# A two-layer deformable convolution kernel: bias sums and image 0's moves in another order, left columns copied by ACT, and one addition moved from POOL to DVE

## The reference, cut to what matters

```
x = x + L0(gn(x))      # L0: a depthwise 3x3 convolution followed by three 32x32 channel mixes
x = x + L1(gn(x))      # L1: deformable: off = conv3x3(x, w_off) gives a row and a column offset per pixel,
                       #     x is sampled bilinearly at (row + off_r, col + off_c), edges clamped,
                       #     the sampled map goes through conv3x3(., w_conv) + b_conv
```

## Time and profile before

| | us |
|---|---|
| median of 3 runs | 744.34 (743.94 to 746.05) |
| the profiled execution | 743.99 |
| its span, first to last instruction | 742.0 |
| PE busy | 688.2 |
| DVE, POOL, ACT busy | 508.1, 491.5, 459.4 |

### The profile page before, as it was taken

One profiled execution on the slowest core, in us unless ns is written; L12 is line 12 of the kernel. 1 busy time (PEld: TensorE's weight loads), 2 busy tenths in 40 slices (PEclk: granted clock), 3 DMA queues, 4 the chain that ended last, 5 costly groups with the idle time before them and its releaser, 6 DMA issues.

```text
span 742.0 us, 10713 instructions
## 1 busy us (share of the span) xinstructions
PE 688.2 (93%) x3500; PEld 249.9 (34%) x3500; DVE 508.1 (68%) x1017; ACT 459.4 (62%) x792; POOL 491.5 (66%) x434
## 2 busy tenths in 40 slices
PE   4799979974999999999999999999999999998955
PEld 4233333321333333333333333333333333333312
DVE  3687897574776688567876688567876675756632
ACT  7576767674556765677556765677557755766520
POOL 4014978697367675867867675866867676799920
PEclk9999999996999999999999999999999999999978
DMA  8959706899859896699849995699849444764484
GB/s 142 187 106 154 113 8 144 176 191 167 177 124 222 172 203 146 166 213 205 175 118 230 182 219 127 160 222 199 184 111 220 105 94 114 172 153 112 91 189 99
DMA packets 140732, 116.70 MB, mean 157 GB/s; under 512 B 15200, under 2 KB 114048, under 8 KB 140672
## 3 DMA queue, kind: packets, MB, share of 16 engines
q1 hardware_dynamic: 116640, 104.18, 66.8%
q10 hardware_dynamic: 24032, 11.78, 8.6%
HBM read 31.59 MB, written 16.78 MB: 65 GB/s over the span
## 4 chain that ended last, share of the span: by engine, by line
PE 65%; SPq 8%; POOL 4%; DMA 3%; DVE 3%; ACT 2%; issue 1%; ACTq 0%; POOLq 0%; DVEq 0%
PE off_ps L762 31%; PE c_ps L651 28%; SPq L375 3%; SPq L456 3%; PE c_ps L662 2%; PE c_ps L666 2%; SPq L479 1%; DMA mapa<-mapped 1%; DMA mapb<-mapa 1%; DMA xb<-xa 1%; DVE other_row L1380 1%; POOL other_col L1182 1%; POOL other_col L1179 1%; POOL mapped L1188 1%; POOL other_col L1177 1%
## 5 line engine op out<-in xcount | busy, mean ns | idle before, releaser
L1380 DVE COPY_PREDICATED other_row<-down_ps,row_diff 128x768 f32<-128x768 int32 x128 | 124.8, 1029 | 134.6 <-ACT down_ps L966 134.6
L762 PE MATMUL off_ps<-x1a,wo 128*64 128x512 f32 x768 | 180.0, 602 | 0.4 <-DVE other_row L1392 0.4
L762 PE MATMUL off_ps<-x1b,wo 128*64 128x512 f32 x768 | 177.0, 593 | 0.0
L1176 POOL TENSOR_TENSOR other_row<-other_row,x_strips 128x512 f32<-128x512 f32 x64 | 76.2, 1190 | 152.1 <-DVE other_row L1392 152.1
L651 PE MATMUL c_ps<-xb,w 128*64 128x512 f32 x336 | 152.3, 603 | 9.1 <-ACT xb L1065 9.1
L653 PE MATMUL c_ps<-xa,w 128*64 128x512 f32 x336 | 152.3, 603 | 0.0
L651 PE MATMUL c_ps<-mapb,w 128*64 128x512 f32 x336 | 150.5, 594 | 0.0
L955 ACT ACTIVATE other_row<-row_diff 128x768 f32<-128x768 f32 x128 | 100.8, 836 | 66.9 <-POOL row_diff L1162 43.4
L653 PE MATMUL c_ps<-mapa,w 128*64 128x512 f32 x294 | 131.4, 594 | 0.0
L966 ACT ACTIVATE down_ps<-off_ps,bias_o 128x512 f32<-128x512 f32 x64 | 41.9, 655 | 123.2 <-PE off_ps L762 116.2
L762 PEld LDWEIGHTS off_ps<-x1b,wo 128*64 128x64 f32 x768 | 56.8, 136 | 110.5 <-issue 110.5
(11 more groups left out here) (133 smaller groups left out, 952.4 us busy)
## 6 DMA issues: line engine op xcount, KB each, us to landing
x1b<-x1a SPq DMA_DIRECT2D x28, 520.0 KB, 6.5
mapa<-mapped SPq DMA_DIRECT2D x224, 65.0 KB, 2.1
mapb<-mapa SPq DMA_DIRECT2D x28, 520.0 KB, 6.8
out_dram<-x1a SPq DMA_DIRECT2D x49, 256.0 KB, 4.8
xb<-in_x_dram SPq DMA_DIRECT2D x48, 256.0 KB, 8.6
xa<-in_x_dram ACTq DMA_DIRECT2D x40, 256.0 KB, 7.2
x_strips<-x1a SPq DMA_DIRECT2D x112, 81.2 KB, 2.1
x_strips<-x1a SPq DMA_DIRECT2D x112, 65.0 KB, 2.1
```

Source lines behind the costliest of these rows:

```text
L762: last = nc.tensor.matmul(off_ps[k % 2][64 * t:64 * t + 64, CH * n:CH * n + CH], wo[wpar][:, kx, side:side + 2 * C], rows[:, b:b + 7:2, kx ...
L1176: step(pool.tensor_tensor(split(column), split(column), own, ALU.add))
L1380: last = dve.copy_predicated(other_row[n][:, :, KR // 2 * odd:KR // 2 * odd + KR // 2, :], bass.AP(tensor=rows.tensor, offset=rows.offset ...
```

## The change

1. The sum `b1` of image 2 goes from behind chunk 4 to chunk 5 of image 0, just ahead of the group `x1` 0 of image 2. `pad_x` of image 2 goes with it, behind chunk 5's `offset_parts` on ACT.
2. The sums `b2` come one or two chunks later than the scaling of their weights on DVE, which stays where it was: chunk 3 in place of 2, and in the last image chunks 2 and 7 in place of 1 and 5.
3. In SP's queue, mapa's first half of image 0 goes ahead of x1b and the strips of image 1, and the strips of image 1's second half go behind x1b's second half.
4. In the last image ACT copies xb's left columns (16 pieces) straight from `mapped` once chunk 5 is mapped; SP's two copies from xa to xb go. ACT, POOL and DVE no longer wait for those before the right columns.
5. In images 0 and 7 DVE adds x1's own rows behind L1392, and POOL leaves L1176 out and waits for DVE (`own_added`) ahead of L1179.

```
-    END_SETUP = 1
-    END_BIAS = 5
-    CONV2_SETUP = 2
+    END_SETUP, END_SETUP_SUM = 1, 2
+    END_BIAS, END_BIAS_SUM = 5, 7
+    CONV2_SETUP, CONV2_SETUP_SUM = 2, 3
     NEXT_BIAS = [6] * NB
-    FURTHER_BIAS = [4] + [NK - 1] * (NB - 1)
+    FURTHER_BIAS = [5] + [NK - 1] * (NB - 1)
+    def added_by_dve(i):
+        return i in (0, NB - 1)
...
             jobs += [("x1", i + 1, m) for m in conv1_groups(i, k)]
+            jobs += [("b1", i + 2, 0)] if i == 0 and k == FURTHER_BIAS[i] else []
             jobs += [("x1", i + 2, m) for m in further_groups(i, k)]
...
                     copy_x1b(i % 3, 1)
+                    if i == 1:
+                        move_strips(sp, i, 1)
                     sp.wait_ge(map_pads, i)
...
+                if not prev:
+                    sp.wait_ge(mapped_ready, 4)
+                    sp.wait_ge(s_setup["dve"], 6)
+                    sp.wait_ge(mapped_pads, 1)
+                    move_mapa(0)
                 if nxt:
...
-                    for half in range(2):
+                    for half in range(2 if prev else 1):
                         move_strips(sp, i + 1, half)
...
                     move_left_columns(end_moved[1])
-                    sp.wait_ge(end_moved[1], A_MOVES * DMA)
-                    copy_rows(xb, xa, 4, 4, end_copied[1])
...
-            act.wait_ge(end_copied[1], B_MOVES * DMA)
+            act.wait_ge(mapped_ready, NK * NB - 2)
+            for q, t, o, shifted in END_ROWS:
+                if shifted:
+                    to, rows = end_row(q, t, o, shifted, slice(0, 1 + WQ))
+                    last = act.activation(to, rows, ACT.Copy)
+            last.then_inc(end_left, 1)
             act.wait_ge(mapped_ready, NK * NB)
...
                     pool.wait_ge(off_used, NK * i + k + 1)
-                    step(pool.tensor_tensor(split(column), split(column), own, ALU.add))
+                    if not added_by_dve(i):
+                        step(pool.tensor_tensor(split(column), split(column), own, ALU.add))
                     step(pool.tensor_tensor(side, side, other_row[n][:, 0, :, :], ALU.add))
                     settle()
+                    if added_by_dve(i):
+                        pool.wait_ge(own_added, own_count(i, k))
...
                 dve.scalar_tensor_tensor(beside, down, bias_o[i % 2][:, :], beside, ALU.add, ALU.mult).then_inc(off_used, 1)
+                if added_by_dve(i):
+                    column = split(other_row[n][:, 1, :, :])
+                    dve.tensor_tensor(column, column, of_chunk(i, k, 1), ALU.add).then_inc(own_added, 1)
```

More of the change, by code:

```diff
@@ L98, in jobs_behind @@
         if i >= 1:
-            jobs += [("b2", i - 1, 0)] if k == (CONV2_SETUP if i + 1 < NB else END_SETUP) else []
+            jobs += [("b2", i - 1, 0)] if k == (CONV2_SETUP_SUM if i + 1 < NB else END_SETUP_SUM) else []
             jobs += [("c2", i - 1, m) for m in (LAST_CONV2 if i + 1 < NB else END_CONV2)[k]]
-        if i + 1 == NB and k == END_BIAS:
+        if i + 1 == NB and k == END_BIAS_SUM:
             jobs += [("b2", i, 0)]
-        if i + 2 < NB and k == FURTHER_BIAS[i]:
+        if 0 < i < NB - 2 and k == FURTHER_BIAS[i]:
             jobs += [("b1", i + 2, 0)]
@@ L246, in deformable_preact_kernel @@
         end_moved = [sem(f"end_rows_moved{n}") for n in range(2)]
-        end_copied = [sem(f"end_rows_copied{n}") for n in range(2)]
+        end_copied = sem("end_rows_copied")
+        end_left = sem("end_left_columns")
         end_rows = {e: sem(f"end_rows_{e}") for e in ("dve", "act", "pool")}
@@ L275, in deformable_preact_kernel @@
         row_selected = sem("row_selected")
+        own_added = sem("own_added")
         col_selected = sem("col_selected")
@@ L332, in end_row @@
             if not shifted:
-                to = xa[Q * q:Q * q + Q, b:b + 4, 1 + WQ:WP]
+                to = xa[Q * q:Q * q + Q, b:b + 4, cols]
             elif q < 2:
-                to = xb[Q * (q + 2):Q * (q + 3), b:b + 4, 1 + WQ:WP]
+                to = xb[Q * (q + 2):Q * (q + 3), b:b + 4, cols]
             else:
-                to = xb[Q * (q - 2):Q * (q - 1), b + 1:b + 5, 1 + WQ:WP]
-            return to, mapped[p:p + Q, q, 4:8, 1 + WQ:WP]
+                to = xb[Q * (q - 2):Q * (q - 1), b + 1:b + 5, cols]
+            return to, mapped[p:p + Q, q, 4:8, cols]
         def stored_count(part, images):
@@ L552, in _ @@
                     sp.wait_ge(end_moved[0], A_MOVES * DMA)
[L553 removed]
+                    copy_rows(xb, xa, 0, 4, end_copied)
                     sp.wait_ge(mapped_pads, 2 * i + 2)
@@ L562, in _ @@
                     break
-                sp.wait_ge(mapped_ready, NK * i + 4)
                 if prev:
+                    sp.wait_ge(mapped_ready, NK * i + 4)
                     sp.wait_ge(conv2_done, 8 * (i - 1) + 4)
[L566 to L569, removed]
+                    sp.wait_ge(mapped_pads, 2 * i + 1)
+                    move_mapa(0)
                 if prev and after:
@@ L1034, in _ @@
                         x1_group(i + 1, (i + 1) % 2, (i + 1) % 3, m, i + 1 >= 3, bank("x1", i + 1, m))
-                    if prev and k == (CONV2_SETUP if nxt else END_SETUP):
+                    if prev and k == (CONV2_SETUP_SUM if nxt else END_SETUP_SUM):
                         conv2_bias(i - 1, (i - 1) % 2, bank("b2", i - 1, 0))
-                    if not nxt and k == END_BIAS + 1:
+                    if not nxt and k == END_BIAS_SUM:
                         conv2_bias(i, i % 2, bank("b2", i, 0))
@@ L1050, in _ @@
                             pad_end(i % 3)
+                    if i == 0 and k == FURTHER_BIAS[i]:
+                        conv1_bias(i + 2, i % 2, bank("b1", i + 2, 0))
                     for m in further_groups(i, k):
@@ L1196, in _ @@
             pool.wait_ge(end_pads, 1)
-            pool.wait_ge(end_copied[1], B_MOVES * DMA)
+            pool.wait_ge(mapped_pads, 2 * NB)
             for which in END_SHARES["pool"]:
@@ L1443, in copy_end_rows @@
             def copy_end_rows():
-                dve.wait_ge(end_copied[1], B_MOVES * DMA)
+                dve.wait_ge(end_pads, 1)
+                dve.wait_ge(mapped_pads, 2 * NB)
                 dve.wait_ge(mapped_ready, NK * NB)
```

11 lines of the change are left out of this document (7 added, 4 removed).

## The result

The changed kernel takes 733.25 us, median of 4 runs (729.92 to 738.49), against 744.31 (743.94 to 746.05): a ratio of 0.986 with a 95% interval of 0.983 to 0.990. The forecast was 721, in a range of 715 to 728: the direction is right, half of the gain is missing, and the time lies outside the range.

What follows compares the result with a forecast made beforehand. PE was taken as the bound, never standing from 184.7 to 633 us, with holes only at both ends. 14.4 + 2.4 - 1.2 + 7.3 = 22.9 us off 743.99 gives 721.1, with 0.35 for the median 721; range 715 to 728.

Steps and rivals of the forecast that it cites:

- SP's order, image 0: Image 0: mapa's first half moved earlier brings mapb at 162.6, wanted at 163.5; 12.7 us hole and 1.7 go, 14.4 us.
- so that stretch only slides: From 184.7 to 633 us PE is busy 448.3 of 448.3 us, its order unchanged, so the stretch only moves earlier.
- a hole at mapb: Sign of being wrong: PE standing for mapb; the forecast expected no hole near 164 and 150 us.
- mapb stays late: Rival, chance 0.18: only 1 us to spare, image 3's loads in the same 10 us; costs 4.1 + 1.7 us, 727.
- the terms: Up to image 0's conv2: 14.4 us from SP's order, 2.4 from conv2's later sums, -1.2 from image 2's bias sum and additions.
- five chunks and five groups: PE's work in image 0 from 124.4 to the end of chunk 4's offsets, put at 38.9 us, so mapb is wanted at 163.5.
- the bound of 9.8 us: Upper bound of the gain at the last image's end, if the loop gains 4.8; then DVE's place counts, 707.9.
- The hole ahead of image 2's `x1` 0: Image 0: PE stands from 98.8 to 104.3 until pad_x, low clock behind; PE's place 1.2 us later.
- The additions on DVE: Images 0 and 7: each costs DVE 0.6 us plus 0 to 1.6 waiting, POOL 0.6 when DVE is first; POOL spared 1.19.
- The end: Last image: wait for SP's left-column copies goes, PE at 710.4 in place of 717.7, 7.3 us; bounds 3.6 to 9.8.
- the end is held by DVE: Rival, chance 0.13: PE's part in the last image comes no earlier, so the end gives 3.6, not 7.3 us: 725.

Runs made afterwards that it cites:

- the end step: An edit: DVE's ten end pieces moved ahead of its addition of image 7's third group; the last hole falls from 4.6 to 2.5 us.
- spread_end: Changed kernel, conv2 of every image in images 6 and 7's order, first store after eight groups, DVE's end pieces one place earlier: 730.63 us, 0.984.

## Why the prediction was right and where it failed

*SP's order, image 0: right.* mapb came in time, and PE began conv2 at 162.85 (forecast 163.5). The moves to mapa stood at 97.1 to 107.9 (forecast 96.5 to 106.7). The gain there was 14.7 us, and nothing of it is missing.

*The step that failed: "so that stretch only slides".* The forecast read 448.3 busy of 448.3 us as a proof that nothing else counts from image 1 to 6. It shows it only at the old distance between PE and SP. A lead of 14.7 us needed SP to be as much earlier in every image, and the prediction put at nothing whatever SP would lose there. In place of sliding, the stretch gave back 12.7 us, in holes for mapb and x1 and in the slow clock behind them. The prediction had itself named a hole at mapb as a sign of being wrong.

SP began image 1's transfers 15.4 us earlier (155.3 against 170.7) and then took 88.1 us to image 1's mapb where it had taken 80.6. Where 5.9 of these 7.5 us come from is in two timelines. Before, ACT's loads of xa were issued while SP ended mapa's moves and then waited for them to land; xb's loads began 8.5 us after the last of those issues:

```profile
160.51 0.97 ACTq L363 DMA_DIRECT2D xa<-in_x_dram  x2
...
162.18 0.70 ACTq L363 DMA_DIRECT2D xa<-in_x_dram  x1
...
170.74 0.64 SPq L470 DMA_DIRECT2D mapb<-mapa  x1
171.42 9.78 SPq L438 DMA_DIRECT2D xb<-in_x_dram  x8
181.30 1.62 SPq L448 DMA_DIRECT2D x1b<-x1a  x1
```

After, both sets of loads are issued together:

```profile
155.32 0.64 SPq L479 DMA_DIRECT2D mapb<-mapa  x1
156.00 15.65 SPq L447 DMA_DIRECT2D xb<-in_x_dram  x8
171.75 2.96 SPq L457 DMA_DIRECT2D x1b<-x1a  x1
...
158.24 2.18 ACTq L372 DMA_DIRECT2D xa<-in_x_dram  x1
```

9.78 us became 15.65, and SP, in order, passed the delay on. The next images go the same way: xb's loads take 15.03, 15.08 and 14.93 us in images 1 to 3, where they took 11.35, 10.52 and 11.40, and 10.88 again in image 4, when the lead is gone and ACT's loads come 5 us behind xb's first. That is 3.5 to 5.9 us an image, as much as the 4 us that SP had to spare. That the two sets of loads slow each other is read from these rows; no run moved one set alone. The rival "mapb stays late" had the right transfer and the wrong image: it asked for the 1 us to spare in image 0 and for no later image. With SP's two consumers relieved the sum comes out: 718.16 plus the 2.1 us of the end step is 720.3, against 721. Some of that agreement is luck: up to image 0's conv2 the gain, with the 1.7 us of slow clock behind it, was 16.4 us where the terms add up to 15.6, and the end brought 5.9 where 7.3 was put.

Slips in the sums change nothing in this: five chunks and five groups are 38.7 us by the prediction's own rows, not 38.9; its chances, with the 0.01 for no change, add up to 1.01; and the place of DVE behind the bound of 9.8 us, 707.9, is given without a working.

*The hole ahead of image 2's `x1` 0: right.* It ended at 103.91 with ACT's padding (forecast 104.3), and the group behind it ran slowly. PE's place was then 0.7 us later than before (forecast 1.2).

*The additions on DVE: right in kind, smaller in price.* Timeline of the changed kernel in image 7, an odd and an even chunk:

```profile
679.69 1.59 POOL L1180 TENSOR_TENSOR row_diff<-x_strips 128x792 f32<-128x792 f32 x1
680.29 1.54 DVE L1418 TENSOR_TENSOR other_row<-other_row,x_strips 128x512 f32<-128x512 f32 x1
681.24 1.34 POOL L1182 TENSOR_TENSOR row_diff<-x_strips 128x330 f32<-128x330 f32 x1
...
695.82 0.68 DVE L1418 TENSOR_TENSOR other_row<-other_row,x_strips 128x512 f32<-128x512 f32 x1
...
695.98 1.65 POOL L1198 TENSOR_TENSOR other_col<-other_col,other_row 128x512 f32<-128x512 f32 x1
```

Alone the addition takes 0.68 (forecast 0.6). Behind POOL's L1180 it takes 1.54: counted back from its end, 681.83 - 0.68, it began at 681.15, when L1180 (to 681.28) was all but done. POOL's L1182 then takes 1.34 where its mean before was 0.90, and L1198 1.65 where it takes 1.27 alone: 0.4 us back for each addition, where 0.6 was put. The exclusion that the prediction took from the Trainium skill, "SBUF — State Buffer", section "Who interferes with whom", agrees with these rows of 512 columns.

*The end: 5.9 us of 7.3.* All is mapped 70.8 us behind image 7's first offsets (701.70), before 73.2: 2.4 us gained, forecast 1.2. But the last hole ended with DVE:

```profile
701.73 0.42 ACT L1085 ACTIVATE xa<-mapped 32x260 f32<-32x260 f32 x1 [1.01 <-POOL mapped L1211]
...
705.23 0.75 DVE L1388 SCALAR_TENSOR_TENSOR x1a<-c_ps,bias,x1a 128x512 f32<-128x512 f32 x1 [1.83 <-PE c_ps L665]
...
706.02 0.35 DVE L1476 TENSOR_SCALAR xa<-mapped,ones 32x260 f32<-32x260 f32 x1
...
709.29 0.35 DVE L1476 TENSOR_SCALAR xb<-mapped,ones 32x260 f32<-32x260 f32 x1
...
709.79 1.09 PE L663 MATMUL c_ps<-xb,w 128*64 128x512 f32 x1 [4.60 <-DVE xb L1476]
```

ACT's wait of 14.55 us is 1.01. DVE's pieces start only behind the third end group's addition, and that came 1.4 us earlier against image 7's first offsets (75.1 us behind them, 76.5 before), where 4.0 was put. PE reached it late: two new holes, 1.54 and 0.48 us, are both ended by DVE's L1388 (the 2.0 us in the waits above). That is the rival "the end is held by DVE" in small; spread_end shows its size, 2 us.

## What to carry to other kernels

An engine that never stands still in a loop is the bound only at the distance that it keeps from the other queues: before a gain ahead of the loop is carried through it, see how much each in-order queue idles per pass, for a lead can become a lasting gain only as far as the slowest queue can follow. Ask also which transfers the new order brings together. Here SP idled some 4 us in an image, and xb's loads beside xa's took 3.5 to 5.9 us longer, so SP could not follow. When a queue is late, look for all who wait on it: relieving one may hand the wait to the next, as it did here, where the whole gain came only when both were relieved.

## What the runs showed of the hardware

SP issues 64 moves of 65 to 81 KB for an image, at 0.63 to 0.82 us apiece (10.91 us for the 16 above): 46 to 48 of the 83 us that PE has for each of images 1 to 4, for the smaller part of the bytes that SP moves. The DMA engines were busy 0.42 of their time meanwhile, by the view by stretches of the changed kernel:

```profile
200.00:211.00 11.00, 11.00 (x70) 4.20 (x68) 6.22 (x10) 4.56 (x7) 10.18 (x9) 1.00 0.42 100
```

SP issued eight loads of 256 KB in 9.78 us behind another queue's loads and in 15.65 beside them. A copy of 520 KB to mapb landed 6.70 us after its issue in one place and 10.0 in another. And the kernels in which SP was late differ by 5 to 10 us from run to run, those that keep the lead by 1 to 3.
